# Sparse attention: four reorderings in a three-stage pipeline, and a list load dropped at the fortieth expert step

## The chip, the cores and the metric

The kernel runs on one core of a Trainium2 chip. The metric is the device time of one execution in microseconds, lower is better; the median of three runs of the kernel before is 567.16 us (565.54 to 567.82).

## The reference

The input is 16 sequences of 256 rows of 128 numbers. Four blocks follow one another, each with a layer norm in front and a residual sum behind: linear attention, a mixture of eight experts, sparse attention, and the same mixture of experts again. Only the sparse attention and a small thing in both expert blocks concern the change. Per sequence (b), cut to what matters:

```
Q, K, V = split(x @ w_qkv.T + b_qkv);  Q, K = rope(Q), rope(K)
iq = (x @ w_iq.T + b_iq)  as 4 heads of 64;  ik = x @ w_ik.T + b_ik;  iw = x @ w_iw.T + b_iw   # 4 weights per row
index_scores = sum over heads of relu(iq_h @ ik.T) * iw_h          # [256, 256]
mask = the 32 largest index_scores of each row
attn = softmax(Q @ K.T / sqrt(128), masked);  out = (attn @ V) @ w_o.T + b_o
```

The expert block sends each row to one of eight experts (a router's argmax) and computes relu(x W1 + b1) W2 + b2, times the gate.

## The kernel before

Each engine has its own instruction stream, and semaphores order them. Every engine executes its stream in order, so the order written in the code is the order of the work.

**Sparse attention** is a software pipeline over the B = 16 sequences. A pass of the loop is a step s; `st.on(lag, B)` says that the step works on sequence s - lag. Each sequence has C = 2 tiles of 128 rows. In a full step:

- Lag -1, the sequence that comes next: ScalarE normalises its rows (`normalise_b`, line 857: two ACTIVATEs, line 864, into `xb`), and copies their transpose out of PSUM (`turned`, line 868, into `xbT`, line 872).
- Lag 0: TensorE transposes `xb` into bank 5 (line 691), and computes seven projections and v in four pairs (`project`, lines 653 to 665; v by line 663) and the head weights iw (lines 712 and 714). ScalarE evicts them (`projected`, line 879: line 888 for the seven, line 891 for v into `vb`; line 915 for iw). GpSimd multiplies the rotation's cosine and sine parts (lines 481 and 483) and adds the two (line 488, `qr`). TensorE computes the index scores of tile c for four heads (`index_scores`, line 673, matmuls of line 679, banks 0 and 1); ScalarE takes the relu (line 927, `rel`), and scales two of the heads by their weights (line 934, `part`); GpSimd adds these two (`add_heads`, line 462, `head_sum`, line 466).
- Lag 1: VectorE adds the third and fourth heads (lines 1274 and 1280, `wk`), then searches the 32 largest in four rounds of MAX8 and MATCH_REPLACE8 (lines 1329 and 1332); ScalarE makes the mask from what was replaced (line 944, `pen`). TensorE computes Q K^T (line 734).
- Lag 2: VectorE adds the mask to the logits (line 1288), ScalarE exponentiates (line 901), TensorE transposes the probabilities into bank 4 (line 670), ScalarE copies them out (line 910, `prT`), and TensorE multiplies them by v (line 724, the value product, bank 7); VectorE adds the residual (line 1250).
- Lags 3 and 4: the layer norm and the router of the next expert block (lines 1262, 522, 751, 508).

`vb` has two buffers. The v of sequence s may be evicted only when the value product of sequence s - 2, which is computed in the same step, has read the buffer: `after(act, b_["PV"], C * (b - 1))` in `projected`.

TensorE's order in a full step is: transpose `xb` of this step's sequence; router; projections 0 to 2; probabilities of tile 0; projection 3; probabilities of tile 1; iw; value product; index scores of tile 0; Q K^T; transpose of the router's rows; index scores of tile 1.

ScalarE's order is: four evictions; two exponentials; router logits; two evictions; `prT`; the last projection; `vb`; iw; `xb` of the next sequence; then per tile two `rel` and two `part`. Behind the first tile's `part` comes the router's `xfT`, between the second tile's `rel` and `part` comes `turned`, and `pen` is last.

**Expert block.** 39 incidences (tile and expert) go through TensorE (lines 629 and 639), ScalarE and VectorE. The tile numbers of the coming steps are loaded from a list in SBUF into VectorE's registers by TENSOR_LOAD (`loaded`, line 295, seen as line 297) at the steps that `opens` names (line 306). VectorE's part lags by two, so its last steps have the numbers 32 to 40; at step 32 it loads nine entries, which are those of steps 32 to 40, and at step 40 it loads again.

Of the kernel before, what the change touches and what calls it, by code (L numbers as in the profile page):

```python
# [11 lines left out]
ACT = mybir.ActivationFunctionType  # L12
AX = mybir.AxisListType

P = 128
B, S, D = 16, 256, 128
C = S // P
T = B * C
# [7 lines left out]
TURN, HEAD = 8, 8  # L26
# [78 lines left out]
def after(eng, sem, count):  # L105

    if not isinstance(count, int) or count > 0:
        eng.wait_ge(sem, count)  # L108
# [11 lines left out]
def build(nc, x, w_attn, w_idx, w_experts, b1_cols, b2, w_router, cols, b_out, b_o, b_iw, b_r, consts, out):  # L120
    with ExitStack() as ctx:  # L121
# [149 lines left out]
        tails = []  # L271
# [33 lines left out]

        def opens(st, lag):

            return (st.base - HEAD) % TURN == 0 or st.base == lag or st.base == T

        block = ctx.enter_context(nc.Block())  # L310

# [58 lines left out]
        def _(pool):  # L370
# [91 lines left out]
            def add_heads(b, r, c):  # L462

                pool.wait_ge(b_["prt"], C * b + c + 1)
                after(pool, b_["s1"], C * (b - 1))
                pool.tensor_tensor(head_sum[r][:, c, :], part[r][:, c, 0, :], part[r][:, c, 1, :],  # L466
                                   ALU.add).then_inc(b_["hs"], 1)
# [9 lines left out]
            for s in range(B + 2):  # L477
                b, r = s, s % 2
                if b < B:
                    pool.wait_ge(b_["pje"], 8 * b + 7)  # L480
                    pool.tensor_tensor(qk[r][:, 0:2, :], qk[r][:, 0:2, :], const("cos").unsqueeze(1).to_broadcast([P, 2, S]),
                                       ALU.mult).then_inc(b_["rp"], 1)
                    pool.tensor_tensor(qk[r][:, 2:4, :], qk[r][:, 2:4, :], const("sin").unsqueeze(1).to_broadcast([P, 2, S]),
                                       ALU.mult).then_inc(b_["rp"], 1)
                    add_heads(b, r, 0)
                    pool.wait_ge(b_["rp"], 2 * (b + 1))
                    after(pool, b_["S"], C * (b - 1))
                    pool.tensor_tensor(qr[r][:, :, :], qk[r][:, 0:2, :], qk[r][:, 2:4, :], ALU.add).then_inc(b_["qr"], 1)
                    add_heads(b, r, 1)
                inverse_std(s)  # L490
                if b < B:
                    pool.wait_ge(b_["xb"], b + 1)
                    pool.tensor_tensor(X[:, b * C:(b + 1) * C, :], X[:, b * C:(b + 1) * C, :],
                                       bo_bc[:, :].unsqueeze(1).to_broadcast([P, C, D]), ALU.add).then_inc(b_["xo"], 1)
                if b + 3 < B:
                    gather_x(b + 3)
# [4 lines left out]
        def _(pe):  # L501
# [9 lines left out]
            def keep_clock(count, where):  # L511

                for i in range(count):
                    pe.transpose(where, ident, ident)
# [134 lines left out]
            pe.wait_ge(ffns[0]["y"], NT)  # L649
            pe.wait_ge(b_["vo"], 2)  # L650
            keep_clock(KEEP_GATHER, bank[4][:, 0:P])
            for st in (Step(s) for s in range(B + 4)):
                def project(pair):

# [27 lines left out]
                        if h >= 2:  # L682
                            mm.then_inc(b_["idx"], 1)

                if st.on(0, B):
                    b, r = st.item(0), st.slot(0, 2)
                    pe.wait_ge(b_["xb"], b + 1)
                    after(pe, b_["iwe"], b)
                    after(pe, tails[1]["xfT"], b - 3)
                    for c in range(C):  # L690
                        mm = pe.transpose(bank[5][:, c * P:(c + 1) * P], xb[r][:, c, :], ident)
                    mm.then_inc(b_["T"], 1)
                if st.on(4, B):

                    after(pe, tails[1]["x"], min(st.item(3) + 1, B) if st.base >= B else st.item(3) + 1)
# [13 lines left out]
                    turn_probabilities(b, r, 1).then_inc(b_["PT"], 1)  # L709
                if st.on(0, B):  # L710
                    b, r = st.item(0), st.slot(0, 2)
                    pe.matmul(bank[5][:, S:S + C * IDX_HEADS], ones[0:1, :], rowc[:, 0:C * IDX_HEADS], start=True, stop=False)
                    for c in range(C):
                        mm = pe.matmul(bank[5][:, S + c * IDX_HEADS:S + (c + 1) * IDX_HEADS], xbT[r][:, c * P:(c + 1) * P],
                                       WB[:, 9 * D:9 * D + IDX_HEADS], start=False, stop=(c == C - 1))
                    mm.then_inc(b_["pj"], 1)
                if st.on(2, B):
                    b, r = st.item(2), st.slot(2, 2)
                    pe.wait_ge(b_["prT"], b + 1)
                    after(pe, tails[1]["x"], b)  # L720
                    after(pe, tails[1]["lg"], b - 1)
                    for c in range(C):
                        for k in range(C):
                            mm = pe.matmul(bank[7][:, c * D:(c + 1) * D], prT[r][:, c, k * P:(k + 1) * P], vb[r][:, k, :],
                                           start=(k == 0), stop=(k == C - 1))
                        mm.then_inc(b_["PV"], 1)
                if st.on(0, B):
                    index_scores(0)
                if st.on(1, B):
# [16 lines left out]
        def _(act):  # L746
# [110 lines left out]
            def normalise_b(st, lag):  # L857

                b, r = st.item(lag), st.slot(lag, 2)
                act.wait_ge(b_["nb"], b + 1)  # L860
                after(act, b_["T"], b - 1)
                for c in range(C):
                    at = bass.ds(b * C + c, 1)
                    ins = act.activation(xb[r][:, c, :], X[:, at, :].rearrange("p a d -> p (a d)"), ACT.Identity,
                                         scale=rs2[r][:, c:c + 1], bias=nb[r][:, c:c + 1])
                ins.then_inc(b_["xb"], 1)

            def turned(b, r):

                act.wait_ge(b_["T"], b + 1)  # L870
                after(act, b_["idx"], 2 * C * (b - 1))
                act.activation(xbT[r][:, :], bank[5][:, 0:S], ACT.Copy).then_inc(b_["xbT"], 1)  # L872

            normalise_b(Step(0), 0)
            turned(0, 0)
            for st in (Step(s) for s in range(B + 4)):
                b, r = st.item(0), st.slot(0, 2)

                def projected(pair):

                    act.wait_ge(b_["pj"], 5 * b + pair + 1)
                    for i in (2 * pair, 2 * pair + 1):
                        src = bank[2 + pair % 2][:, i % 2 * S:(i % 2 + 1) * S]
                        if i == 3:
                            after(act, b_["qr"], b - 1)
                        if i < 7:
                            dst = iq[r][:, i, :] if i < 2 else ik[r][:, :] if i == 2 else qk[r][:, (0, 2, 1, 3)[i - 3], :]
                            act.activation(dst, src, ACT.Identity, bias=COL[:, 2 + i:3 + i]).then_inc(b_["pje"], 1)  # L888
                        else:
                            after(act, b_["PV"], C * (b - 1))  # L890
                            act.activation(vb[r][:, :, :], src.rearrange("p (c d) -> p c d", c=C), ACT.Copy).then_inc(b_["pje"], 1)
# [17 lines left out]
                    after(act, b_["PV"], C * (p - 1))  # L909
                    act.activation(prT[q][:, :, :], bank[4][:, :].rearrange("p (c k) -> p c k", c=C), ACT.Copy).then_inc(b_["prT"], 1)  # L910
                if st.on(0, B):
                    projected(3)
                    act.wait_ge(b_["pj"], 5 * (b + 1))
                    after(act, b_["wk"], C * (b - 1))
                    act.activation(iw[r][:, :, :],
                                   bank[5][:, S:S + C * IDX_HEADS].rearrange("p (c h) -> p c h", c=C),
                                   ACT.Copy).then_inc(b_["iwe"], 1)
                if st.on(-1, B):
                    normalise_b(st, -1)
                for c in range(C):  # L920
                    if st.on(0, B):
                        if c == 0:
                            after(act, b_["hs"], C * (b - 1))
                            act.wait_ge(b_["iwe"], b + 1)
                        for i in range(2):
                            act.wait_ge(b_["idx"], 2 * (C * b + c) + i + 1)
                            act.activation(rel[r][:, c, i::2, :],  # L927
                                           bank[i][:, :].rearrange("p (h k) -> p h k", h=2), ACT.Relu).then_inc(b_["rel"], 1)
                    if c == C - 1 and st.on(-1, B):
                        turned(st.item(-1), st.slot(-1, 2))  # L930
                    if st.on(0, B):
                        act.wait_ge(b_["rel"], 2 * (C * b + c + 1))
                        for h in range(2):
                            ins = act.activation(part[r][:, c, h, :], rel[r][:, c, h, :], ACT.Copy,  # L934
                                                 scale=iw[r][:, c, h:h + 1])
                        ins.then_inc(b_["prt"], 1)
                    if c == 0 and st.on(3, B):
                        xf_out(1, st.item(3), st.slot(3, 2), bank[5][:, 0:S])
                if st.on(1, B):
# [449 lines left out]
```

## Time and profile before

| | |
|---|---|
| median of 3 runs (range) | 567.16 us (565.54 to 567.82) |
| the profiled execution's own time | 566.95 us |
| its span, first to last instruction | 565.1 us |
| mean granted TensorE clock | 0.922 of full speed |
| busy: TensorE, VectorE, ScalarE, GpSimd | 80%, 67%, 60%, 51% of the span |

The sparse attention runs from about 215 to 413 us of the span, the expert blocks before and after it. Busy shares are means over stages with different limits; the stage's own rows say more. In rows of a timeline the first number is the start, the second the duration (several instructions of one kind that follow one another are merged: x2), and the bracket is the idle time of the engine before it with what ended it.

### The profile page before, as it was taken

Reading aid. Unit: us, or ns where it says so; the run is one execution under the profiler, and the core shown is the slowest. Engines: PE = TensorE matmul, PEld = TensorE weight load, DVE = VectorE, ACT = ScalarE, POOL = GpSimd, SP = SyncE. Lnnn points to the kernel's source line nnn. Section 1 sums busy time; section 2 is a strip of 40 time slices with the busy share of each in tenths; the row PEclk is TensorE's granted clock in tenths of the full one; section 3 lists DMA queues with packets and bytes.
Section 4 is the critical chain, followed back from the end, with each engine's and each line's share of the span. In section 5 each row is a group of like instructions: output and inputs, shape, how many; then the busy total and the mean of one; then the engine's idle time right before and its main releaser. Section 6 shows DMA issues by size and latency. Waiting matters only on the chain. (4 is left out here: it accounts for less than half of the span.)

```text
span 565.1 us, 11633 instructions
## 1 busy us (share of the span) xinstructions
PE 451.0 (80%) x3048; PEld 390.7 (69%) x3048; DVE 380.0 (67%) x1501; ACT 337.2 (60%) x934; POOL 288.4 (51%) x329
## 2 busy tenths in 40 slices
PE   1789985859999986999889998889647668786991
PEld 1578865859999874676666766667437568676981
DVE  5789976425666622999999999999957234434661
ACT  1568852226776616889999899998521245434650
POOL 5753440454430025987778777775410633665442
PEclk9989995979999989999999999999756969888996
DMA  8942232131331110011111111110111321121110
GB/s 224 288 135 77 74 90 25 44 88 53 99 87 35 34 34 15 9 37 32 28 30 30 42 44 28 30 30 21 36 35 5 84 57 48 56 64 56 39 36 17
DMA packets 45070, 32.42 MB, mean 57 GB/s; under 512 B 13524, under 2 KB 39508, under 8 KB 45012
## 3 DMA queue, kind: packets, MB, share of 16 engines
q1 hardware_dynamic: 39892, 19.11, 12.2%
q0 software_dynamic: 5120, 12.62, 8.5%
q8 instruction: 26, 0.43, 0.3%
q14 instruction: 32, 0.26, 0.2%
HBM read 19.10 MB, written 12.62 MB: 56 GB/s over the span
## 5 line engine op out<-in xcount | busy, mean ns | idle before, releaser
L629 PE MATMUL bank<-X,w 128*128 x624 | 91.0, 292 | 18.3 <-ACT X L834 16.3
L639 PE MATMUL bank<-WE,hT 128*128 x624 | 89.2, 289 | 14.3 <-ACT hT L847 6.8
L427 POOL DMA_INDIRECT big<-rows,gidx x64 | 61.5, 961 | 74.7 <-DVE gidx L1147 28.2
L629 PEld LDWEIGHTS bank<-X,w 128*128 128x128 f32 x624 | 82.0, 205 | 22.3 <-issue 21.9
L639 PEld LDWEIGHTS bank<-WE,hT 128*128 128x128 f32 x624 | 81.3, 203 | 17.0 <-issue 16.9
L834 ACT ACTIVATE X<-bank 128x128 f32<-128x128 f32 x64 | 17.9, 280 | 94.6 <-PE bank L620 60.9
L1179 DVE TENSOR_SCALAR hT<-bank,w 128x128 f32<-128x128 f32 x156 | 47.6, 346 | 39.0 <-issue 12.2
L660 PE MATMUL bank<-xbT,WB 128*128 128x256 f32 x224 | 59.2, 394 | 13.2 <-ACT xbT L872 8.5
L839 ACT ACTIVATE w<-WE 128x644 f32 x78 | 57.5, 738 | 3.1 <-DVE big L1191 2.8
L847 ACT ACTIVATE hT<-bank,w 128x128 f32<-128x128 f32 x156 | 48.7, 367 | 13.4 <-PE bank L629 10.1
L447 POOL DMA_INDIRECT X<-x,pidx x32 | 31.7, 989 | 48.7 <-DMA x<-big 41.2
L660 PEld LDWEIGHTS bank<-xbT,WB 128*128 128x128 f32 x224 | 38.7, 189 | 25.2 <-ACT iq L888 11.1
L1332 DVE MATCH_REPLACE8 wk<-m,wk 128x256 f32<-128x256 f32 x128 | 51.8, 416 | 0.0
L433 POOL DMA_INDIRECT out<-big,gidx x32 | 31.4, 980 | 38.1 <-DVE big L1191 32.5
L1329 DVE MAX8 m<-wk 128x8 f32<-128x256 f32 x128 | 47.9, 419 | 0.0
L1185 DVE TENSOR_TENSOR yb<-bank,w 128x128 f32<-128x128 f32 x78 | 22.6, 289 | 36.3 <-PE bank L639 20.4
L1191 DVE SCALAR_TENSOR_TENSOR big<-yb,gm,big 128x128 f32 x78 | 27.5, 353 | 16.4 <-DVE yb L1185 12.1
L679 PE MATMUL bank<-ik,iq 64*128 64x256 f32 x256 | 37.8, 402 | 0.7 <-ACT big L927 0.7
L466 POOL TENSOR_TENSOR head_sum<-big 128x256 f32<-128x256 f32 x32 | 23.6, 736 | 27.9 <-ACT big L934 27.8
L927 ACT ACTIVATE big<-bank 128x512 f32<-128x512 f32 x64 | 34.7, 594 | 1.1 <-PE bank L679 0.9
L888 ACT ACTIVATE big<-bank,COL 128x256 f32<-128x256 f32 x64 | 29.4, 496 | 0.8 <-PE bank L660 0.7
L934 ACT ACTIVATE big<-big,iw 128x256 f32<-128x256 f32 x64 | 29.3, 511 | 0.6
(161 smaller groups left out, 1026.6 us busy)
## 6 DMA issues: line engine op xcount, KB each, us to landing
WE<-w_experts SPq DMA_DIRECT2D x2, 2048.0 KB, 11.5
rows<-xf SPq DMA_DIRECT2D x32, 128.0 KB, 2.2
rows<-X SPq DMA_DIRECT2D x32, 128.0 KB, 2.7
X<-x SPq DMA_DIRECT2D x4, 512.0 KB, 7.6
x<-big SPq DMA_DIRECT2D x32, 64.0 KB, 1.5
big<-rows,gidx POOLq DMA_INDIRECT x64
WB<-w_idx SPq DMA_DIRECT2D x1, 640.0 KB, 5.7
WE<-b SPq DMA_DIRECT2D x1, 512.0 KB, 12.9
```

What stands on the lines that cost most here:

```text
L427: pool.indirect_dma_start(xg[:, j, :], None, rows_dram[n], bass.IndirectOffsetOnAxis(ap=gidx[:, j:j + 1], axis=0)).then_inc(f["g"][j % G_R ...
L447: pool.indirect_dma_start(X[:, t, :], None, x2_dram, bass.IndirectOffsetOnAxis(ap=pidx[:, t:t + 1], axis=0)).then_inc(b_["x"][r], 16)
L629: mm = pe.matmul(bank[r + 2 * (k // 2)][:, k % 2 * P:(k % 2 + 1) * P], w1[st.slot(1, 4)][:, k * P:(k + 1) * P], moving, start=True, stop=True)
L639: mm = pe.matmul(bank[4 + r][:, 0:D], hT[r][:, k, :], WE[:, bass.ds(expert[(s - 2) % TURN], 1), W2_AT + k * D:W2_AT + (k + 1) * D].rearran ...
L660: mm = pe.matmul(to, WB[:, i * D:(i + 1) * D], xbT[r][:, :], start=True, stop=True)
L679: mm = pe.matmul(bank[h % 2][:, h // 2 * S:(h // 2 + 1) * S], iq[r][lo:lo + IDX_DIM, h // 2, c * P:(c + 1) * P], ik[r][lo:lo + IDX_DIM, :] ...
L839: act.activation(w1[st.slot(0, 4)][:, :], WE[:, bass.ds(expert[st.base], 1), 0:W1_LEN].rearrange("p a w -> p (a w)"), ACT.Copy).then_inc(f ...
L847: act.activation(hT[r][:, k, :], bank[r][:, k * P:(k + 1) * P], ACT.Relu, bias=w1[st.slot(1, 4)][:, B1_AT + k:B1_AT + k + 1]).then_inc(f[" ...
L927: act.activation(rel[r][:, c, i::2, :], bank[i][:, :].rearrange("p (h k) -> p h k", h=2), ACT.Relu).then_inc(b_["rel"], 1)
L1179: dve.tensor_scalar(hT[r][:, k, :], bank[2 + r][:, k % 2 * P:(k % 2 + 1) * P], w1[st.slot(1, 4)][:, B1_AT + k:B1_AT + k + 1], 0.0, ALU.add ...
L1329: dve.max(m8[:, c, :], wk[r][:, c, :]).then_inc(b_["v"], 1)
L1332: dve.match_replace(wk[r][:, c, :], m8[:, c, :], wk[r][:, c, :], NEG).then_inc(b_["v"], 1)
```

## The change

1. TensorE transposes the rows of sequence s + 1 in step s, behind the value product and ahead of the index scores of tile 0, into bank 4 instead of bank 5. The first sequence's are transposed ahead of the loop.
2. ScalarE's order behind `prT` becomes: last projection, `xb` of the next sequence, iw, `vb`. `turned` moves from between the second tile's `rel` and `part` to behind the first tile's `part`, ahead of `xfT`.
3. GpSimd adds the rotation's parts (line 488) ahead of both `add_heads`, not between them.
4. `opens` names no step beyond 32, so VectorE's list load at step 40 goes, in both expert blocks.

```diff
         def opens(st, lag):
-            return (st.base - HEAD) % TURN == 0 or st.base == lag or st.base == T
+            return st.base <= T and ((st.base - HEAD) % TURN == 0 or st.base == lag or st.base == T)
@@ gpsimd
-                    add_heads(b, r, 0)
                     pool.wait_ge(b_["rp"], 2 * (b + 1))
                     after(pool, b_["S"], C * (b - 1))
                     pool.tensor_tensor(qr[r][:, :, :], qk[r][:, 0:2, :], qk[r][:, 2:4, :], ALU.add).then_inc(b_["qr"], 1)
+                    add_heads(b, r, 0)
                     add_heads(b, r, 1)
@@ tensor
+            def turn_rows(b, r):
+                pe.wait_ge(b_["xb"], b + 1)
+                for c in range(C):
+                    mm = pe.transpose(bank[4][:, c * P:(c + 1) * P], xb[r][:, c, :], ident)
+                mm.then_inc(b_["T"], 1)
+            turn_rows(0, 0)
             for st in (Step(s) for s in range(B + 4)):
...
-                if st.on(0, B):
-                    b, r = st.item(0), st.slot(0, 2)
-                    pe.wait_ge(b_["xb"], b + 1)
-                    after(pe, b_["iwe"], b)
-                    after(pe, tails[1]["xfT"], b - 3)
-                    for c in range(C):
-                        mm = pe.transpose(bank[5][:, c * P:(c + 1) * P], xb[r][:, c, :], ident)
-                    mm.then_inc(b_["T"], 1)
...
                 if st.on(0, B):
                     b, r = st.item(0), st.slot(0, 2)
+                    after(pe, tails[1]["xfT"], b - 3)
                     pe.matmul(bank[5][:, S:S + C * IDX_HEADS], ones[0:1, :], rowc[:, 0:C * IDX_HEADS], start=True, stop=False)
...
                         mm.then_inc(b_["PV"], 1)
+                if st.on(-1, B):
+                    turn_rows(st.item(-1), st.slot(-1, 2))
                 if st.on(0, B):
                     index_scores(0)
@@ scalar
-                act.activation(xbT[r][:, :], bank[5][:, 0:S], ACT.Copy).then_inc(b_["xbT"], 1)
+                act.activation(xbT[r][:, :], bank[4][:, 0:S], ACT.Copy).then_inc(b_["xbT"], 1)
...
-                def projected(pair):
+                def projected(pair, which=(0, 1)):
...
-                    projected(3)
+                    projected(3, (0,))
+                if st.on(-1, B):
+                    normalise_b(st, -1)
+                if st.on(0, B):
                     act.wait_ge(b_["pj"], 5 * (b + 1))
                     ...
-                if st.on(-1, B):
-                    normalise_b(st, -1)
+                if st.on(0, B):
+                    projected(3, (1,))
...
-                    if c == C - 1 and st.on(-1, B):
-                        turned(st.item(-1), st.slot(-1, 2))
                     if st.on(0, B):
                         act.wait_ge(b_["rel"], 2 * (C * b + c + 1))
                         ...
+                    if c == 0 and st.on(-1, B):
+                        turned(st.item(-1), st.slot(-1, 2))
```

## Rows read from the trace of the kernel before

**Rows 1.** Busy in one full step: length, PE, PEld, DVE, ACT, POOL; clock, DMA.

```profile
308.77:320.61 11.84, 10.68 (x66) 8.18 (x64) 11.17 (x47) 10.53 (x31) 9.33 (x11) 1.00 0.14 35
```

**Rows 2.** Waits from 260 to 380 us: who waited for whom, sum, times, longest.

```profile
ACT vb L891 <- PE bank L724: 8.8, 10, 0.9
...
DVE lg L1288 <- ACT pen L944: 5.5, 11, 0.5
```

**Rows 3.** Timeline of one full step: start, us, engine, line, operation.

```profile
309.82 0.87 ACT L888 ACTIVATE big<-bank,COL 128x256 f32<-128x256 f32 x2
...
310.97 0.17 DVE L1237 SCALAR_TENSOR_TENSOR nb<-mv,rs 128x2 f32<-128x2 f32 x1
...
311.09 0.60 ACT L910 ACTIVATE prT<-bank 128x512 f32<-128x512 f32 x1 [0.39 <-PE bank L670]
...
311.58 0.47 ACT L888 ACTIVATE big<-bank,COL 128x256 f32<-128x256 f32 x1
...
311.76 1.14 PE L724 MATMUL bank<-vb,prT 128*128 128x128 f32 x8
...
312.83 1.13 PE L679 MATMUL bank<-ik,iq 64*128 64x256 f32 x8
312.94 0.39 ACT L891 ACTIVATE vb<-bank 128x256 f32<-128x256 f32 x1 [0.88 <-PE bank L724]
...
313.28 0.88 ACT L864 ACTIVATE xb<-X,nb,rs 128x128 f32<-128x128 f32 x2
...
314.08 1.09 ACT L927 ACTIVATE big<-bank 128x512 f32<-128x512 f32 x2
...
315.20 0.91 ACT L934 ACTIVATE big<-big,iw 128x256 f32<-128x256 f32 x2
...
316.01 0.36 ACT L751 ACTIVATE xfT<-bank 128x256 f32<-128x256 f32 x1
...
316.34 1.09 ACT L927 ACTIVATE big<-bank 128x512 f32<-128x512 f32 x2
...
316.49 0.20 PEld L691 LDWEIGHTS bank<-cst,xb 128*128 128x128 f32 x2 [0.55 <-issue]
...
316.77 0.51 PE L508 MATMUL bank<-WR,xfT 128*128 128x8 f32 x4
...
317.31 0.39 ACT L872 ACTIVATE xbT<-bank 128x256 f32<-128x256 f32 x1
...
317.57 0.92 ACT L934 ACTIVATE big<-big,iw 128x256 f32<-128x256 f32 x2
```

**Rows 4.** The same step's end: GpSimd's rotation sum, VectorE's first head sum.

```profile
316.87 1.27 POOL L488 TENSOR_TENSOR qr<-big 128x512 f32<-128x512 f32 x1
...
317.39 1.03 DVE L1274 SCALAR_TENSOR_TENSOR wk<-big,iw,head_sum 128x256 f32<-128x256 f32 x1
```

**Rows 5.** Timeline of the first two steps, in which no value product runs yet.

```profile
221.06 1.13 PE L679 MATMUL bank<-ik,iq 64*128 64x256 f32 x8
...
222.28 1.09 ACT L927 ACTIVATE big<-bank 128x512 f32<-128x512 f32 x2 [0.17 <-PE bank L679]
...
226.78 0.84 ACT L888 ACTIVATE iq<-bank,COL 128x256 f32<-128x256 f32 x2 [0.42 <-PE bank L660]
...
229.88 0.16 DVE L1237 SCALAR_TENSOR_TENSOR nb<-mv,rs 128x2 f32<-128x2 f32 x1
```

**Rows 6.** VectorE's list load in the first expert block: minimum, median, maximum ns, starts.

```profile
L297 DVEq TENSOR_LOAD <-ti x1: 1918/1918/1918, 201.2 to 201.2; - x1
```

**Rows 7.** Timeline of that end.

```profile
199.75 2.13 PE L639 MATMUL bank<-WE,hT 128*128 x15
...
203.48 0.28 DVE L1185 TENSOR_TENSOR yb<-bank,w 128x128 f32<-128x128 f32 x1
```

**Rows 8.** Timeline of the end of the second expert block.

```profile
550.75 2.24 PE L639 MATMUL bank<-WE,hT 128*128 x16
...
554.60 0.28 DVE L1185 TENSOR_TENSOR yb<-bank,w 128x128 f32<-128x128 f32 x1
```

More of the change, by code:

```diff
@@ L877, in _ @@
                 b, r = st.item(0), st.slot(0, 2)
-                def projected(pair):
+                def projected(pair, which=(0, 1)):
                     act.wait_ge(b_["pj"], 5 * b + pair + 1)
-                    for i in (2 * pair, 2 * pair + 1):
+                    for i in (2 * pair + w for w in which):
                         src = bank[2 + pair % 2][:, i % 2 * S:(i % 2 + 1) * S]
```

## The prediction

> **What bounds the kernel now.** I read the busy time of one full step first [rows 1]: 11.84 us, in which VectorE is busy 11.17, TensorE 10.68 and ScalarE 10.53, at the full granted clock. No engine fills the step, so it is a loop of waits that sets it. The waits come second [rows 2]: ScalarE stands 0.88 us ahead of v's eviction in every full step, until the value product has ended, and VectorE stands 0.5 us until ScalarE has made the mask. The reader is to see the direction: VectorE waits for ScalarE and ScalarE waits for TensorE, and ScalarE never waits for VectorE. VectorE's high share is thus not the bound. Third, the timeline gives the loop [rows 3]: ScalarE's first exponential starts at 308.77; TensorE turns the probabilities, and `prT` starts at 311.09 (2.32, with 0.39 of waiting); TensorE multiplies by v (311.76 to 312.90) and computes the index scores of tile 0 (from 312.83); the first `rel` starts at 314.08 (2.99 behind `prT`); from there ScalarE works with hardly a gap to the next first exponential at 320.61 (6.53). The three add up to 11.84.
>
> The important reading is at 312.83. The first `rel` needs these index scores, and in the first step, where nothing else holds ScalarE, it starts 1.22 behind their start (221.06 to 222.28, with a wait [rows 5]). So in the full step they are ready at 312.83 + 1.22 = 314.05, and `rel` starts at 314.08. Behind the wait for the value product a second wait for TensorE lies, only 0.03 us shorter.
>
> **Part 1 and 2, the order on TensorE and ScalarE.** Moving v's eviction behind `xb` and iw fills the 0.88 us, but whatever ScalarE does there, it can't start `rel` ahead of the index scores, and those now stand behind two transposes, which in turn wait for `xb`. Step by step from `prT` at 311.09 [rows 3]:
> - The last projection's eviction starts at 311.58. Two such evictions in a row take 0.87 with 0.51 for the last, so the next instruction may start 0.36 later, at 311.94. The two `xb` take 0.88: they end at 312.82. Their input nb doesn't hold them up: VectorE writes it by 311.14 [rows 3].
> - TensorE has ended the value product at 312.90 by the model of its ends. The transposes start about 0.05 behind `xb` (the value product starts 0.07 behind the end of `prT`, 311.69 to 311.76): 312.87.
> - The two transposes hold TensorE from 316.49 to 316.77 today, 0.28. They end at 313.15, and with 0.09 for the change to the scores' form of matmul the scores start at 313.24 where it was 312.83. (The 0.09 is an estimate: of the value product's eight matmuls, 1.14 in all with 0.28 for one, the last begins near 312.63 and frees the array near 312.74, and the scores start at 312.83.)
> - `rel` starts at 313.24 + 1.22 = 314.46 instead of 314.08: **+0.38**. ScalarE has evicted iw and v by about 313.3 and stands until then. The 0.88 of idle time isn't gone; it now lies ahead of `rel`, and is longer.
>
> Queued behind the new wait of TensorE for `xb` are the scores of tile 0, Q K^T, the router's transposes and the scores of tile 1; ScalarE waits for the first.
>
> `turned` moves too. Before, from the first `rel` to the third (314.08 to 316.34) are 2.26, of which ScalarE could have spared a little: the copy `xfT` is followed 0.33 later, where `xbT` of the same size is followed after 0.26. With `turned` ahead of `xfT` it is 1.12 (to `part`) + 0.81 (two `part`) + 0.26 + 0.26 = 2.45: +0.19. From the third `rel` to the next `part` it was 1.23 with `turned` between; without it, it is the 1.12 that the first pair shows: -0.11. Net **+0.08**, so a full step costs 0.46 more: 12.30.
>
> The earlier `xbT` lets TensorE begin the projections without the 0.5 us it idles today. That is worth nothing: ScalarE's evictions are reached in order, later than the products are ready. The waits removed or moved (for iw, and for `xfT`) had ended long before.
>
> How many steps: full steps with a next sequence are 2 to 14. In step 2 there is no `xfT` yet, so `turned` costs about nothing: 0.38. Steps 3 to 14: 12 x 0.46 = 5.5. Steps 0 and 1 have no value product to wait for, so there the transposes land wholly on the path. In step 0 the last eviction starts at 220.32 (estimated: 0.36 ahead of v's at 220.69), `xb` ends at 221.56, the scores start at 221.56 + 0.05 + 0.28 + 0.09 = 221.98 instead of 221.06: +0.92, and +0.15 from `turned`; 0.5 of it is taken up by the wait at 226.78 [rows 5]. In step 1 `xb` now comes early enough to wait for VectorE's nb (229.88 to 230.04), which hangs on step 0's `part` and so comes 1.07 later, 231.11; `xb` then ends at 232.03 and the scores start at 232.45 instead of 230.46: 2.0 behind in all. Sum for the stage: 2.0 + 0.4 + 5.5 = **7.9 us**. From both sides: 0, if the transposes hide in TensorE's gaps; 0.44 each time for the transposes with their drain and 0.1 for waits that I can't see, which makes 0.72 a full step, 2.0 + 13 x 0.72 = 11.4.
>
> **Part 3, the rotation sum.** Today it starts at 316.87 and VectorE's first head sum, begun at 317.39, takes 1.03 [rows 4] where others take 0.48. Moved ahead, it runs about 314.7 to 316.0, while VectorE searches maxima, which the cosine and sine products lie beside already. `part` ends at about the same time as today, so `add_heads` isn't late. This frees about 0.5 of VectorE, which then waits 0.5 longer for the mask: 0. Past no DMA is it moved, for the gathers stand at the end of GpSimd's step.
>
> The Trainium skill (SBUF — State Buffer, "SBUF: two separate sides") says that VectorE with two SBUF inputs and GpSimd reading SBUF exclude each other for a whole instruction; the trace agrees with its 1.03. By that rule alone the change is a gain of 0.5 a step.
>
> **Part 4, the list load.** It takes 1.92 us on VectorE's queue from 201.2 [rows 6]. TensorE's last product ends at 199.75 + 2.13 = 201.88 [rows 7], and its sum starts at 203.48 only; 0.04 behind the product it would start at 201.92: 1.56 earlier. In the second block 550.75 + 2.24 = 552.99, 553.03 instead of 554.60: 1.57 [rows 8]. The first block's last store and the second's last scatter wait for just these sums. Nothing runs beside either. Sum **-3.1**; bounds -2.6 to -3.8 (twice the load's own 1.92).
>
> **Sum.** 566.95 + 7.9 - 3.1 = 571.75 for the profiled execution, which is 0.2 below the median of 567.16. I say 571.8.
>
> **Rivals.**
> - *The gap in front of v goes and doesn't come back (faster).* For: it is the largest wait of the stage. Then 14 full steps give 0.88 each, 566.95 - 12.3 - 3.1 = 551.5. It needs index scores that are ready at 313.2, while today's come at 314.05 with nothing between them and the value product. It decides where the scores start: 0.03 of slack speaks against it. 0.05.
> - *VectorE sets the pace after all, and the rotation sum gives it back.* 14 x 0.5 = 7: 566.95 - 7 - 3.1 = 556.9. For: 11.17 of 11.84 busy. Against: VectorE waits for the mask in each step. 0.04.
> - *The transposes hide.* If TensorE finds `xb` ready earlier and overlaps them, the stage stays as it is: 563.8. For: two transposes are only 0.28. Against: TensorE issues in order, and the value product leaves no gap. 0.11.
> - *Half the cost*, 0.2 a step and a milder start: 566.95 + 4.2 - 3.1 = 568.1. 0.10.
> - [...] 0.05.
>
> Mine has 0.65. I count as no change what lies within 0.5% (2.8 us). Slower: 0.65 + 0.05. Same: 0.10 and half of the hidden case, 0.16. Faster: 0.14. The range goes from 566.5, a little below half the cost, to 575.5, near the upper bound (575.3).
>
> **What would show it.** Right: ScalarE's wait ahead of L891 shrinks to 0.1 or so, and one of about 1.2 us ahead of the first L927, ended by TensorE's L679, stands in its place; the step is 12.2 to 12.4 long; VectorE waits about 1 us or more for the mask at its L1288, and no L1274 takes 1 us; both list loads are gone and the last sums start 1.6 earlier. Wrong: a step under 11.84, or ScalarE waiting for VectorE.

## The result, and the profile after

The changed kernel takes 572.71 us (median of 4 runs, 571.13 to 573.67) against 566.35 (median of 4, 565.2 to 567.82): ratio 1.0108, 95% interval 1.0071 to 1.0145. A repetition (c1 below) gave 572.56 against 567.38, ratio 1.009 (1.0058 to 1.0123). It is slower, as forecast (571.8), and by about the forecast size: +4.8 us was forecast over the profiled execution of the kernel before, and the medians differ by 6.4 and 5.2. All ratios compare undisturbed executions only; one of the kernel before, beside f1, took 848.71 us and is in none of them. The profiled execution took 571.13 us with a span of 569.3, at a mean granted clock of 0.924.

A full step of the sparse attention, in the view of busy time (length; busy TensorE, weight loads, VectorE, ScalarE, GpSimd; granted clock; DMA), and the waits from 264 to 384 us:

```profile
299.75:312.06 12.31, 10.75 (x66) 8.14 (x65) 10.65 (x47) 10.63 (x31) 9.40 (x11) 1.00 0.12 32
```

```profile
ACT big L933 <- PE bank L687: 11.0, 10, 1.1
ACT prT L913 <- PE bank L678: 4.0, 10, 0.4
...
DVE lg L1294 <- ACT pen L950: 13.0, 9, 1.5
```

Against [rows 1] the step has grown from 11.84 to 12.31. No engine works much more in it: TensorE, ScalarE and GpSimd are busy 0.07 to 0.10 us longer, VectorE 0.52 shorter. What has grown is the waiting. Against [rows 2] the wait of 0.88 ahead of v's eviction is gone, and one of 1.1 ahead of the first `rel` (now line 933), ended by the index scores (now line 687), stands in its place. VectorE waits up to 1.5 for the mask where it waited up to 0.5.

The timeline of that step, which answers to [rows 3] and [rows 4] (line 656 is the transposes' new place, 867 `xb`, 894 v, 875 `xbT`, 754 `xfT`, 938 `part`, 487 the rotation sum, 1280 the first head sum):

```profile
302.03 0.60 ACT L913 ACTIVATE prT<-bank 128x512 f32<-128x512 f32 x1 [0.39 <-PE bank L678]
...
302.53 0.47 ACT L891 ACTIVATE big<-bank,COL 128x256 f32<-128x256 f32 x1
...
302.71 1.14 PE L725 MATMUL bank<-vb,prT 128*128 128x128 f32 x8
...
302.88 0.88 ACT L867 ACTIVATE xb<-X,nb,rs 128x128 f32<-128x128 f32 x2
...
303.82 0.44 PE L656 MATMUL bank<-cst,xb 128*128 128x128 f32 x2
303.94 0.39 ACT L894 ACTIVATE vb<-bank 128x256 f32<-128x256 f32 x1
...
304.19 1.13 PE L687 MATMUL bank<-ik,iq 64*128 64x256 f32 x8
...
305.43 1.09 ACT L933 ACTIVATE big<-bank 128x512 f32<-128x512 f32 x2 [1.10 <-PE bank L687]
...
305.72 1.27 POOL L487 TENSOR_TENSOR qr<-big 128x512 f32<-128x512 f32 x1
...
306.55 0.92 ACT L938 ACTIVATE big<-big,iw 128x256 f32<-128x256 f32 x2
...
307.37 0.36 ACT L875 ACTIVATE xbT<-bank 128x256 f32<-128x256 f32 x1
...
307.63 0.37 ACT L754 ACTIVATE xfT<-bank 128x256 f32<-128x256 f32 x1
307.90 1.08 ACT L933 ACTIVATE big<-bank 128x512 f32<-128x512 f32 x2
...
308.38 0.48 DVE L1280 SCALAR_TENSOR_TENSOR wk<-big,iw,head_sum 128x256 f32<-128x256 f32 x1
...
309.01 0.91 ACT L938 ACTIVATE big<-big,iw 128x256 f32<-128x256 f32 x2
```

Read it as a queue on TensorE: the value product starts at 302.71, the transposes at 303.82 (0.06 behind the end of `xb` at 303.76), the index scores at 304.19. The scores start 2.16 behind `prT`, where before it was 1.74 (311.09 to 312.83). ScalarE has v out by 304.33 and then stands until 305.43.

The end of both expert blocks, which answers to [rows 7] and [rows 8] (now line 1191 is the last sum's first half, 1197 its second):

```profile
199.27 1.46 PE L639 MATMUL bank<-WE,hT 128*128 x9
...
200.77 0.29 DVE L1191 TENSOR_TENSOR yb<-bank,w 128x128 f32<-128x128 f32 x1 [0.26 <-PE bank L639]
```

```profile
556.77 1.90 PE L639 MATMUL bank<-WE,hT 128*128 x13
...
558.72 0.29 DVE L1191 TENSOR_TENSOR yb<-bank,w 128x128 f32<-128x128 f32 x1 [0.27 <-PE bank L639]
```

The sum starts 0.04 and 0.05 behind the end of TensorE's last product (200.73 and 558.67) where it was 1.60 and 1.61. The loads are gone.

And the stage's first projections, 14 matmuls in both kernels. The view of the kernel before:

```profile
215.29 0.44 PE L691 MATMUL bank<-cst,xb 128*128 128x128 f32 x2 [2.65 <-ACT xb L864]
216.21 3.63 PE L660 MATMUL bank<-xbT,WB 128*128 128x256 f32 x14 [0.47 <-ACT xbT L872]
```

The same of the changed kernel:

```profile
212.43 0.44 PE L656 MATMUL bank<-cst,xb 128*128 128x128 f32 x2 [3.98 <-ACT xb L867]
213.34 5.09 PE L668 MATMUL bank<-xbT,WB 128*128 128x256 f32 x14 [0.47 <-ACT xbT L875]
```

This is a cost that the prediction doesn't have: 5.09 instead of 3.63, 1.46 us. It isn't the same in every trace of the kernel before. Its second trace (c2), and two of the experiments below that keep the list load (e2 and e3), have, in this order:

```profile
214.65 4.98 PE L660 MATMUL bank<-xbT,WB 128*128 128x256 f32 x14 [0.47 <-ACT xbT L872]
...
216.89 3.62 PE L660 MATMUL bank<-xbT,WB 128*128 128x256 f32 x14 [0.47 <-ACT xbT L872]
...
216.94 3.62 PE L660 MATMUL bank<-xbT,WB 128*128 128x256 f32 x14 [0.47 <-ACT xbT L872]
```

So with the load three traces of four have 3.6; the ten traces without it have 4.95 to 5.41.

From the traces, the distance of the first `rel` of each step from that of the step before (us). The last three columns are experiments e2, e3 and e4 below. Second traces of the kernel before and of the changed kernel have 11.82 and 12.29 in steps 4 to 14, so a step length repeats to 0.02.

| step | before | changed | v last alone | rotation alone | rows behind the scores |
|---|---|---|---|---|---|
| 1 | 9.41 | 10.40 | 9.39 | 9.39 | 8.99 |
| 2 | 11.57 | 11.97 | 11.57 | 11.56 | 11.61 |
| 3 | 11.62 | 12.03 | 11.61 | 11.60 | 11.64 |
| 4 to 14, mean | 11.84 | 12.31 | 11.83 | 11.82 | 11.89 |
| 15 | 11.84 | 11.90 | 11.83 | 11.82 | 11.89 |

### The profile page after: what moved, and what is told of

It is laid out like the page before. It is cut to its first block and busy times, and to the rows that moved or that the text cites. A ratio compares the mean times of both kernels' runs of the same rounds, so it can differ in the third digit from the quotient of the medians.

```text
span 569.3 us, 11630 instructions
## 1 busy us (share of the span) xinstructions
PE 451.1 (79%) x3048; PEld 389.0 (68%) x3048; DVE 371.3 (65%) x1501; ACT 338.1 (59%) x934; POOL 288.9 (51%) x329
## 5 line engine op out<-in xcount | busy, mean ns | idle before, releaser
L668 PE MATMUL bank<-xbT,WB 128*128 128x256 f32 x224 | 60.4, 401 | 16.1 <-ACT iq L891 15.3
L668 PEld LDWEIGHTS bank<-xbT,WB 128*128 128x128 f32 x224 | 40.0, 195 | 27.7 <-ACT iq L891 21.3
L687 PEld LDWEIGHTS bank<-ik,iq 64*128 64x128 f32 x256 | 23.9, 186 | 7.6 <-ACT big L933 4.2
## 6 DMA issues: line engine op xcount, KB each, us to landing
WE<-w_experts SPq DMA_DIRECT2D x2, 2048.0 KB, 11.7
```

Source lines behind the costliest of these rows:

```text
L668: mm = pe.matmul(to, WB[:, i * D:(i + 1) * D], xbT[r][:, :], start=True, stop=True)
L687: mm = pe.matmul(bank[h % 2][:, h // 2 * S:(h // 2 + 1) * S], iq[r][lo:lo + IDX_DIM, h // 2, c * P:(c + 1) * P], ik[r][lo:lo + IDX_DIM, :] ...
```

## The experiments

Each kernel was timed beside the kernel before on the same chip; all comparisons are with that.

**e1, the list load alone.**

```diff
-            return (st.base - HEAD) % TURN == 0 or st.base == lag or st.base == T
+            return st.base <= T and ((st.base - HEAD) % TURN == 0 or st.base == lag or st.base == T)
```

> The kernel before with only the list load at step 40 left out (part 4). Theory: each load stands alone on the path at the end of its expert block, so both go whole: the last sum of each block starts 1.6 us earlier, in all -3.1 us, 563.2 against 566.35. The sparse attention stays at 11.84 us a step. Rival, one of the two is covered (by the last store or scatter): -1.6. Rival, both are covered: 0.

Measured: 565.61 against 567.47, ratio 0.9962 (0.9938 to 0.9986), which is -2.2 us (the medians differ by 1.9). In its trace the second half of each last sum starts 0.54 and 0.53 behind TensorE's last product (2.09 and 2.11 before), so each load's delay went whole, about 1.56 each. But the stage's first projections take 5.1 us here too:

```profile
215.72 5.12 PE L660 MATMUL bank<-xbT,WB 128*128 128x256 f32 x14 [0.47 <-ACT xbT L872]
```

The theory is right in place and wrong in sum: against the first trace of the kernel before, 1.5 us are given back at the start of the next stage. It was repeated as c3:

> The kernel before without the list load at step 40, once more, since the first interval (-0.62% to -0.14%) held both -3.1 us and less. Theory: -3.1 us, and in the trace the last sum of each block starts 0.5 us behind TensorE's last product instead of 2.1. Rival, part of it is covered: -1.6 us, one of the two last sums still 2 us behind.

Measured: 565.19 against 567.38, ratio 0.9978 (0.9956 to 1.0), which is -1.2 us (the medians differ by 2.2); both last sums 0.5 behind, and the first `rel` again 9.40 behind the first `xb` (7.93 in the first trace of the kernel before). -3.1 + 1.5 = -1.6 lies in both intervals, -3.1 in the first alone.

**e2, ScalarE's order alone.**

```diff
-                    projected(3)
+                    projected(3, (0,))
+                if st.on(-1, B):
+                    normalise_b(st, -1)
+                if st.on(0, B):
                     act.wait_ge(b_["pj"], 5 * (b + 1))
...
-                if st.on(-1, B):
-                    normalise_b(st, -1)
+                if st.on(0, B):
+                    projected(3, (1,))
```

> The kernel before with only ScalarE's order changed behind prT: last projection, xb, iw, v (the transposes and their copy stay where they were). Theory: the wait of 0.88 us ahead of v's eviction goes, but the first rel still waits for the tile-0 index scores, which TensorE starts 1.74 us behind the start of prT as before; a wait of about 0.8 us stands ahead of the first rel instead, the step is 11.81 to 11.84 us, and the time moves by 0 to -0.5 us. Rival, the gap goes and doesn't come back: 10.96 us a step, -12 us.

Measured: 567.42 against 567.47, ratio 1.0001 (0.9975 to 1.0026); step 11.83. The wait has moved and the step hasn't changed; this refutes the rival "the gap goes and doesn't come back". ScalarE and TensorE in one step of its trace:

```profile
311.68 0.60 ACT L910 ACTIVATE prT<-bank 128x512 f32<-128x512 f32 x1 [0.39 <-PE bank L670]
...
313.42 1.13 PE L679 MATMUL bank<-ik,iq 64*128 64x256 f32 x8
313.59 0.38 ACT L891 ACTIVATE vb<-bank 128x256 f32<-128x256 f32 x1
...
314.67 1.09 ACT L930 ACTIVATE big<-bank 128x512 f32<-128x512 f32 x2 [0.69 <-PE bank L679]
```

The scores start 1.74 behind `prT` and `rel` 2.99 behind it, exactly as before the change. Of the 0.88, 0.69 shows again as a wait ahead of `rel` and 0.12 as idle time ahead of v.

**e3, the rotation sum alone.**

```diff
-                    add_heads(b, r, 0)
                     pool.wait_ge(b_["rp"], 2 * (b + 1))
                     after(pool, b_["S"], C * (b - 1))
                     pool.tensor_tensor(qr[r][:, :, :], qk[r][:, 0:2, :], qk[r][:, 2:4, :], ALU.add).then_inc(b_["qr"], 1)
+                    add_heads(b, r, 0)
                     add_heads(b, r, 1)
```

> The kernel before with only GpSimd's rotation sum ahead of both head sums (part 3). Theory: VectorE's first head sum falls from 1.03 to 0.48 us, its wait for the mask grows from 0.5 to about 1.05 us, the step stays at 11.84 us and the time doesn't move (within 0.3 us). Rival, VectorE sets the pace: 11.3 us a step, -7 us.

Measured: 567.0 against 567.47, ratio 0.9988 (0.9969 to 1.0007); step 11.82. The wait and the head sums of its trace (count, minimum/median/maximum ns):

```profile
DVE lg L1288 <- ACT pen L944: 11.1, 11, 1.1
```

```profile
L1274 DVE SCALAR_TENSOR_TENSOR wk<-big,iw,head_sum x21: 450/483/485, 260.8 to 379.0; 128x256 f32<-128x256 f32 x21
```

The stretched head sums (up to 1.08 in the kernel before) are gone, and VectorE gives all of it to its wait for the mask. The rival that VectorE sets the pace is refuted.

**e4, the transposes behind the scores.** The changed kernel with one thing moved:

```diff
-                if st.on(-1, B):
-                    turn_rows(st.item(-1), st.slot(-1, 2))
                 if st.on(0, B):
                     index_scores(0)
+                if st.on(-1, B):
+                    turn_rows(st.item(-1), st.slot(-1, 2))
```

> The changed kernel with the next rows' transposes behind the tile-0 index scores instead of ahead of them; nothing else differs. Theory: the scores start again 1.74 us behind the start of prT instead of 2.16, so the first rel comes 0.4 us earlier; Q K^T, the router's transposes and with them the tile-1 scores come 0.25 later, which gives 0.1 back. Step 11.9 to 12.0 instead of 12.31 us, the first two steps' 2 us mostly gone: about 565 us against 572.7. Rival, the slowdown comes from the order on ScalarE or from the moved copy of the transposed rows: step 12.2 to 12.3, 572.

Measured: 566.47 against 567.47, ratio 0.9981 (0.9961 to 1.0001); step 11.89, the first step even shorter than before (8.99). The two transposes and their wait for `xb`, ahead of the scores, are the slowdown: with them behind the scores 0.42 of the 0.47 a step are gone, while ScalarE's new order is still in place. Refuted are the rival of this run and the prediction's "the transposes hide". One step of its trace:

```profile
310.56 0.60 ACT L913 ACTIVATE prT<-bank 128x512 f32<-128x512 f32 x1 [0.40 <-PE bank L678]
...
312.30 1.13 PE L687 MATMUL bank<-ik,iq 64*128 64x256 f32 x8
...
313.54 1.09 ACT L933 ACTIVATE big<-bank 128x512 f32<-128x512 f32 x2 [0.69 <-PE bank L687]
```

Scores at 1.74 and `rel` at 2.98 behind `prT` again. The sum came out 1.5 us above the expected 565, but that was reckoned from 566.35 for the kernel before, which took 567.47 here: against it -1.4 was expected and -1.0 measured. The slow first projections are in this trace too (5.03 us).

**e5, the transposes twice.** `for c in (0, 1, 0, 1):` in place of `for c in range(C):` in `turn_rows`.

> The changed kernel with the next rows transposed twice (four transposes in place of two, the second pair writes the same values again). Theory: transposes at this place lie on the path with their whole time, 0.25 to 0.28 us for two: step 12.56 to 12.59 instead of 12.31 us, about +4 us (577). Rival, it is only the new wait for xb that costs and the transposes hide: step 12.31, no change.

Measured: 537.24 against 528.83 (ratio 1.018, 1.0143 to 1.0216; on these times see below); step 12.51, +0.20. The second pair lies on the path but costs 0.2 instead of 0.25: in a row, 4 take 0.66 where 2 take 0.44.

```profile
307.73 0.66 PE L656 MATMUL bank<-cst,xb 128*128 128x128 f32 x4
```

So of the change's 0.42 delay of the scores about half is the transposes themselves. The rest is put down to the wait for `xb` (0.16 idle ahead of their weight load) and the start behind it; no run separates these two. The expected total of 577 can't be checked, for the changed kernel wasn't run in this condition.

**e6, the copy of the rows back in its gap.**

```diff
+                    if c == C - 1 and st.on(-1, B):
+                        turned(st.item(-1), st.slot(-1, 2))
                     if st.on(0, B):
                         act.wait_ge(b_["rel"], 2 * (C * b + c + 1))
...
-                    if c == 0 and st.on(-1, B):
-                        turned(st.item(-1), st.slot(-1, 2))
```

> The changed kernel with ScalarE's copy of the transposed rows back between the second tile's rel and part. Theory: the copy hides there in the gap between rel and part, 0.09 us a step, and nothing needs it earlier: step 12.22 instead of 12.31 us, about -1 us. Rival, the earlier copy lets TensorE start the projections earlier and is worth something: step above 12.31 us.

Measured: 532.82 against 528.83, ratio 1.0087 (1.0054 to 1.0121); step 12.22 as expected, 0.09 under the first trace of the changed kernel and 0.07 under its second. The total can't resolve 1 us against the changed kernel's 1.0108 and 1.009; the step length can.

**e7, the scores ahead of the value product.**

```diff
+                if st.on(0, B):
+                    index_scores(0)
                 if st.on(2, B):
                     b, r = st.item(2), st.slot(2, 2)
                     pe.wait_ge(b_["prT"], b + 1)
...
-                if st.on(0, B):
-                    index_scores(0)
```

> The changed kernel with the tile-0 index scores ahead of the value product; v is still evicted ahead of the first rel. Theory: the scores are ready early, but v's eviction now waits for a value product that ends at 3.0 us behind the start of prT, and the first rel follows at 3.3 instead of 3.40: step 12.2 us. ScalarE waits ahead of v again, for 1.2 us or so, and not ahead of rel. Rival, only the place of the scores counts: 11.4 us or less.

Measured: 531.2 against 528.83, ratio 1.0053 (1.0026 to 1.008); step 12.24, with `rel` 3.34 behind `prT` (expected 3.3). The rival, 11.4 or less, is refuted. ScalarE's longest wait is ahead of v:

```profile
ACT vb L894 <- PE bank L727: 10.2, 8, 1.3
```

The two waits of ScalarE are for two products of one in-order engine. Whichever is evicted first must be computed first; moving one of both only changes which wait is seen.

**e9, both orders turned together.** Beyond e7: v evicted behind the first tile's `part`, tile-1 scores ahead of Q K^T, `xfT` behind the second `part`, the router behind the third projection pair (and VectorE's mask waits for both tiles of Q K^T, which share a bank). ScalarE's part of the edit:

```diff
-                if st.on(0, B):
-                    projected(3, (1,))
...
+                    if c == 0 and st.on(0, B):
+                        projected(3, (1,))
                     if c == 0 and st.on(-1, B):
                         turned(st.item(-1), st.slot(-1, 2))
-                    if c == 0 and st.on(3, B):
+                    if c == C - 1 and st.on(3, B):
                         xf_out(1, st.item(3), st.slot(3, 2), bank[5][:, 0:S])
```

> A reordering drawn from the loop: index scores of tile 0 ahead of the value product, v evicted behind the first tile's part, tile-1 scores ahead of Q K^T, the router's copy xfT behind the second tile's part and the router behind the third pair of projections, the rest as in the changed kernel. Theory: the first rel starts at about 1.96 us behind the start of prT (3.40 in the changed kernel), the second tile's rel at 4.5, the mask at 6.7 instead of 7.3 in the kernel before: step 11.3 us, near VectorE's own 10.8 us, about 556 to 558 us. Rival, TensorE's order becomes the bound (it is busy 10.7 us a step): 11.8 us or more.

Measured: 517.14 against 528.83, ratio 0.9786 (0.9759 to 0.9813), -11.7 us; step 11.19. One step:

```profile
309.71 0.60 ACT L913 ACTIVATE prT<-bank 128x512 f32<-128x512 f32 x1 [0.43 <-PE bank L678]
...
310.45 1.13 PE L687 MATMUL bank<-ik,iq 64*128 64x256 f32 x8
...
311.52 1.16 PE L727 MATMUL bank<-vb,prT 128*128 128x128 f32 x8
...
311.70 1.08 ACT L931 ACTIVATE big<-bank 128x512 f32<-128x512 f32 x2 [0.20 <-PE bank L687]
...
313.63 0.36 ACT L894 ACTIVATE vb<-bank 128x256 f32<-128x256 f32 x1
```

`rel` starts 1.99 behind `prT` (expected 1.96), while the value product runs, and v is taken out without a wait. The step in the view of busy time:

```profile
307.38:318.57 11.19, 10.14 (x66) 8.17 (x65) 11.02 (x47) 10.49 (x31) 9.27 (x11) 1.00 0.12 35
```

VectorE is busy 11.02 of the 11.19 us: a further gain on TensorE or ScalarE alone can be 0.17 a step at most, unless VectorE's own work shrinks. By the ratios this version beats both kernels. It moves several things at once, and no run tells them apart.

**c1 and c2, the changed kernel and the kernel before again,** since e5 to e9 ran where the kernel before takes 529 us.

> The changed kernel, beside the kernel before and the list-only kernel on one chip, since the last four kernels ran where the kernel before takes 528.8 us and not 567. Theory: the cost lies in the attention's order of work and is the same in microseconds there: step 12.31 us, +4 to +6 us over the kernel before, whatever that takes. Rival, the cost is tied to the slower expert blocks of the first measurements: a ratio within 0.3% of 1.

> The kernel before, for its trace in the state that its runs now have. Theory: attention step 11.83 us as in the first trace; the difference between 567 and 529 us lies in the expert blocks alone, in pauses of several us that the first trace has and this one has not. Rival: every stage is a little faster.

Measured: 572.56 against 567.38, and 565.58 for the single execution of c2. Neither ran in the quicker condition, so whether the cost in microseconds is the same there wasn't measured; the step lengths of e5 to e7, which follow the theory, speak for it. The steps repeat: 12.29 and 11.82.

**f1, e9 with 84 transposes ahead of the stage** (`KEEP_ROUTE, KEEP_GATHER = 32, 84` for 32, 60).

> The reordered kernel e9_scores_first with 84 instead of 60 of the transposes that keep TensorE busy ahead of the stage (KEEP_GATHER). In the traces without the list load TensorE ends these 60 in 6.8 us at the full clock, stands 4 us, and then runs the first projections at half the clock: 14 of them take 5.1 us where they took 3.6 in the kernel before, in which the 60 lasted 8.3 us and the gap 2.65. Theory: the clock of the first projections depends on TensorE's gap ahead of them; with 24 more transposes of 0.11 us the gap shrinks to about 1.3 us, the 14 take 3.6 us again, and the time falls by 1.4 us against e9. Rival, the clock follows something else: 5.1 us, no gain. For the whole kernel: about 0.9765 of the kernel before, 554 us where that takes 567, or 516 where it takes 529.

Measured: 515.63 against 528.41, ratio 0.976 (0.9732 to 0.9788). The first projections:

```profile
202.43 0.44 PE L656 MATMUL bank<-cst,xb 128*128 128x128 f32 x2 [1.37 <-ACT xb L867]
203.34 5.06 PE L668 MATMUL bank<-xbT,WB 128*128 128x256 f32 x14 [0.47 <-ACT xbT L875]
```

The gap shrank to 1.37 and they still take 5.06 us (5.41 in e9). The theory that the gap sets the clock fell in this trace; whether the whole is 0.3% faster than e9 the intervals don't say.

## Why the prediction was right

- **The bound.** Right: a loop between ScalarE and TensorE, with VectorE following. e3 freed VectorE and e2 removed ScalarE's largest wait, and neither moved the step. TensorE kept its full granted clock in the step (1.00 in both kernels).
- **The second wait behind the first,** 0.03 us shorter. Right, and the step on which all else hung: e2's step is 11.83, between the 11.84 and 11.82 of the kernel before's two traces.
- **The scores' delay.** Predicted +0.41 at the scores and +0.38 at `rel`; measured +0.42 (2.16 for 1.74) and +0.41 (3.40 for 2.99). `turned`: predicted +0.08, measured 0.07 to 0.09 by e6. A full step: 12.30 predicted, 12.31 and 12.29 measured; e4 shows the cause.
- **The first steps.** Predicted 2.0 behind at step 1. In step 0, `rel` is 10.31 behind the first `xb` instead of 7.93: 2.38, of which 1.46 is the slower clock, so 0.92 as predicted for the transposes (the prediction lets a wait take up 0.5, where its row [rows 5] shows 0.42; the sum doesn't hang on it). Step 1 adds 0.99, which makes 1.91. The wait for nb came as said (0.36 us). The stage: 0.92 + 0.99 + 0.40 + 0.41 + 11 x 0.47 + 0.06 = 7.95, predicted 7.9.
- **The rotation sum.** Predicted 0; the medians of e3 differ by 0.5 us, and the interval of its ratio holds 1. The head sum fell from 1.03 to 0.48 us. The Trainium skill ("SBUF — State Buffer", section "SBUF: two separate sides") has VectorE, with two inputs in SBUF, and GpSimd exclude each other on a shared port for a whole instruction; the trace agrees with its 1.03 and 0.48. The step doesn't follow: VectorE isn't what bounds it.
- **The list load.** Predicted -3.1. The term is right where it stands (-1.55 and -1.57), but it lacks what comes next: in all ten traces without the load the first projections take 4.95 to 5.41 us, and 3.6 in three of the four with it. With it the sum is 7.95 - 3.1 + 1.5 = 6.3 against the first trace (6.0 against the mean of the four), and the medians differ by 6.4 and 5.2.
- **Luck in the total.** The forecast of 571.8 lies only 0.9 under the median, though the missing term is 1.5: it started from 566.95, and the median of the kernel before turned out as 566.35.

That the changed profile's own time is only 4.2 above that of the kernel before comes from other stages and isn't explained: the last sum of the first expert block starts 2.71 us earlier, where the load explains 1.56.

## What to carry to other kernels

A wait is worth at most what the next wait on the same engine leaves of it: before filling a gap, compute when the consumer behind it could start, for here filling 0.88 us of idle time gained nothing that the step length shows. On an in-order engine, place what the slow partner waits for next ahead of all that it doesn't, and move producer and consumer together: e7, which moved the producer alone, was 0.5% slower than the kernel before, and e9 took 2.1% off. And read step lengths out of the trace where a loop repeats: they agreed to 0.02 us between traces of one kernel, while 0.3% of the whole, 1.7 us, was noise.

## What the runs showed of the hardware

**TensorE's clock at a stage's start.** The 60 transposes ahead of the stage, the gap, and the first step, in the view of busy time of the kernel before (start:end, length, engines, granted clock):

```profile
204.40:212.70 8.30, 8.24 (x60) 8.00 (x60) 0.43 (x2) 0.00 (x0) 3.78 (x4) 0.81 0.15 40
212.70:215.30 2.60, 0.01 (x1) 0.01 (x1) 1.20 (x8) 0.88 (x2) 1.90 (x3) 1.00 0.03 8
215.30:222.30 7.00, 6.35 (x34) 4.71 (x34) 0.90 (x5) 4.62 (x13) 3.35 (x6) 1.00 0.07 19
```

The same of the changed kernel:

```profile
201.70:208.45 6.75, 6.75 (x60) 6.50 (x60) 0.05 (x1) 0.00 (x0) 3.19 (x4) 1.00 0.13 37
208.45:212.35 3.90, 0.00 (x0) 0.00 (x0) 1.46 (x9) 0.86 (x2) 3.12 (x5) 1.00 0.19 48
212.35:221.80 9.45, 8.26 (x36) 6.06 (x36) 0.90 (x5) 4.50 (x13) 3.64 (x5) 0.82 0.03 9
```

With the load, TensorE stood longer ahead of the 60 (2.50 us for 0.94), ran them at a granted 0.81, and had the full 2.4 GHz for the first step. Without it, it ran them at 1.00 and then had 0.82 in the first step, about half of the 14 projections at the 1.2 GHz level (0.63 us each for 0.38). The second trace of the kernel before has 0.84 and then 0.79 with nearly the gaps of the first (2.50 and 2.77), and f1 has 1.00 and then the slow projections after a gap of 1.37 only. So neither the load nor the gap alone sets it; what does stays open.

**Two levels of the whole.** The kernel before took 567.5, 567.4 and, in two other sets of runs, 528.8 and 528.4 us; one chip showed both. No kernel was profiled in both, but the one step that the changed kernel and e5 have alike, step 15, takes 11.90 in the slower condition and 11.89 in the quicker. Most of the difference lies in the expert blocks: in the second one the sums take 98.7 us from first to last in the kernel before's first trace and 77.4 in e6's. ScalarE's waits in the slower one have a part that no instruction of the program ends (440 to 520 us, the changed kernel):

```profile
ACT X L837 <- remote: 15.1, 3, 9.2
```

A wait of this kind, 9.3 us long, stands at the start of the first block too (from 112 to 122 us); e6 has none in either place.

None of the runs tells where these pauses come from. No result above rests on them, since each ratio is with the kernel before on the same chip.
